# Contracting a bias matmul over 33 partitions instead of 128, in a fused cross-attention and expert kernel

## The reference, cut to what matters

```python
q = (layernorm(x) @ Wq + bq).reshape(1, B * N, H, hd)     # 1024 tokens, 16 heads of 32
kv = (cond @ Wkv + bkv).reshape(1, -1, 2, H, hd)          # 2048 context tokens
k, v = kv[:, :, 0], kv[:, :, 1]
q, k = _fq_sym(q * scale, axis=-1), _fq_sym(k, axis=-1)   # rounded to 255 levels
v = _fq_sym(v, axis=2)
attn = _fq_unsigned(softmax(q k^T))
x = x + (attn @ v) @ Wp + bp
x = x + sum over 8 experts of weight_e * ((silu(xn @ Wg_e) * (xn @ Wu_e)) @ Wd_e)
```

## Time and profile before

| | us |
|---|---|
| median of 3 runs | 724.55 |
| lowest and highest of the 3 | 721.7, 725.01 |
| the profiled execution, its own time | 725.01 |
| its span, first to last instruction | 723.2 |

### The profile page before, as it was taken

One profiled execution on the slowest core, in us unless ns is written; L12 is line 12 of the kernel. 1 busy time (PEld: TensorE's weight loads), 2 busy tenths in 40 slices (PEclk: granted clock), 3 DMA queues, 4 the chain that ended last, 5 costly groups with the idle time before them and its releaser, 6 DMA issues.

```text
span 723.2 us, 15795 instructions
## 1 busy us (share of the span) xinstructions
PE 618.9 (86%) x5307; PEld 328.3 (45%) x5307; DVE 567.9 (79%) x926; ACT 462.1 (64%) x559; POOL 402.8 (56%) x455
## 2 busy tenths in 40 slices
PE   6999999666867777777777688799999999999995
PEld 3444444233434333443434356455555555555543
DVE  4998888999999999999999998783646547465430
ACT  6344459789979989898989898343434334344321
POOL 5255458537587878787877874234334453344503
PEclk9999999999999999999999999899999999999998
DMA  7777857999989999999999999269697787967914
GB/s 254 198 148 176 182 135 145 182 190 194 173 165 198 184 198 193 188 192 189 189 189 185 200 176 170 88 213 212 162 253 161 225 221 176 242 157 225 145 27 58
DMA packets 318516, 129.42 MB, mean 179 GB/s; under 512 B 293508, under 2 KB 293508, under 8 KB 318472
## 3 DMA queue, kind: packets, MB, share of 16 engines
q1 hardware_dynamic: 311296, 112.64, 72.8%
q0 software_dynamic: 7168, 16.26, 11.0%
q10 hardware_dynamic: 8, 0.01, 0.0%
HBM read 44.33 MB, written 12.06 MB: 78 GB/s over the span
## 4 chain that ended last, share of the span: by engine, by line
PE 46%; issue 14%; DVE 11%; POOL 8%; DMA 7%; ACT 7%; SPq 5%; POOLq 1%; another core or an unknown queue 0%; ACTq 0%; DVEq 0%
PE psum L1668 43%; DMA work<-work 7%; ACT work L1065 4%; DVE spare L1400 3%; POOL work L672 3%; DVE spare L1391 2%; SPq L483 2%; SPq L481 2%; POOL exp_bias L678 1%; PE psum L1987 1%; SPq L450 1%; ACT work L967 1%; POOL work L657 1%; POOL bias_hl L636 1%; POOL out_dram L846 1%
## 5 line engine op out<-in xcount | busy, mean ns | idle before, releaser
L1065 ACT ACTIVATE work<-spare,exp_bias 128x2048 uint8<-128x2048 f32 (+1 forms) x127 | 253.2, 1995 | 29.3 <-POOL exp_bias L678 21.8
L1400 DVE TENSOR_SCALAR_CACHE_REDUCE spare<-psum,q_step_now 128x1024 f32<-128x1024 f32 x128 | 162.8, 1279 | 2.7 <-PE psum L1839 2.5
L672 POOL CAST work<-work 128x2048 int16<-128x2048 uint8 x70 | 132.3, 1890 | 39.2 <-DMA work<-work 35.4
L1391 DVE TENSOR_SCALAR_CACHE_REDUCE spare<-psum,q_step_now 128x2048 f32<-128x2048 f32 x64 | 150.6, 2353 | 0.1
L1839 PE MATMUL psum<-keys_region,work 128*128 128x512 f16 x256 | 73.1, 385 | 43.0 <-DVE spare L1400 27.1
L834 POOL DMA_INDIRECT work<-x_rows,slot_tok x32 | 49.8, 1558 | 88.5 <-DVE slot_w L1600 75.1
L1839 PE MATMUL psum<-keys_region,bias_hl 128*128 128x512 f16 x256 | 70.6, 381 | 28.4 <-DVE spare L1400 22.9
L846 POOL DMA_INDIRECT out_dram<-keys_region,slot_tok x32 | 51.7, 1615 | 74.8 <-ACT keys_region L1160 67.8
L1798 PEld LDWEIGHTS psum<-values_region,work 128*128 128x128 f16 x2016 | 65.0, 96 | 36.5 <-POOL work L672 21.6
L1668 PE MATMUL psum<-work,spare 128*128 128x480 f16 (+1 forms) x396 | 80.5, 364 | 0.0
L1798 PE MATMUL psum<-values_region,work 128*128 128x32 f16 x2016 | 70.0, 177 | 10.8 <-POOL work L672 7.0
(11 more groups left out here) (250 smaller groups left out, 1005.4 us busy)
## 6 DMA issues: line engine op xcount, KB each, us to landing
spare<-in_L_ffn_Wd_dram SPq DMA_DIRECT2D x8, 1024.0 KB, 15.5
spare<-in_L_ffn_Wg_dram SPq DMA_DIRECT2D x7, 1024.0 KB
spare<-in_L_ffn_Wu_dram SPq DMA_DIRECT2D x7, 1024.0 KB, 10.3
work<-in_ctx_dram SPq DMA_DIRECT2D x3, 1024.0 KB, 5.8
work<-work SPq DMA_TRANSPOSE x174, 3.7
token_region<-in_L_xattn_Wkv_dram SPq DMA_DIRECT2D x2, 1024.0 KB, 6.1
resid<-in_x_dram SPq DMA_DIRECT2D x2, 1024.0 KB, 8.9
out_dram<-work SPq DMA_DIRECT2D x8, 256.0 KB, 2.6
```

Source lines behind the costliest of these rows:

```text
L672: nc.gpsimd.tensor_copy(p_T_int[h % 4], pair_bytes[h % 4]).then_inc(unpacked, 1)
L1065: nc.scalar.activation(p_out, scores, ACT.Exp, bias=exp_bias[:, h % 4:h % 4 + 1], scale=-1.0, accum_out=p_sum[:, h:h + 1]).then_inc(exp_do ...
L1391: nc.vector.tensor_scalar(staged[h % 4], psum[:, at:at + 4, :].rearrange("p b k -> p (b k)"), q_step_now[:, h:h + 1], None, ALU.mult, ALU.min,
L1400: nc.vector.tensor_scalar(staged[h % 4][:, 1024 * c:1024 * c + 1024], psum[:, at:at + 2, :].rearrange("p b k -> p (b k)"), q_step_now[:, h ...
```

## The change

`add_bias` reads partitions 0 to 32 of both operands and leaves partitions 33 to 127 out. Nothing else is edited: the two operands are still cleared whole, `warm_up` still reads the whole of `bias_one`, and every semaphore stays where it was. The output still has 128 rows and 512 columns. What was added from the rows left out was zero times zero.

```diff
             def add_bias(out, n):
 
-                return nc.tensor.matmul(out, bias_one[:, :], bias_hl[:, n, :], start=False, stop=True)
+                return nc.tensor.matmul(out, bias_one[0:33, :], bias_hl[0:33, n, :], start=False, stop=True)
```

## The result

The changed kernel is slower: the ratio to the kernel before, over 8 runs of each, is 1.0063 with a 95% interval of 1.0035 to 1.0093. On the 725.08 us median of the kernel before that is 4.6 us, 2.5 to 6.7 by the interval. The medians themselves are 728.38 and 725.08 us, 3.3 us apart. The profiled execution took 731.33 us with a span of 729.6, which is the high end of its runs, as the profiled one of before was for the first three shown.

What follows compares the result with a forecast made beforehand. TensorE was taken to bound the front: 22 bias matmuls x 0.26 us, less 0.24 us of slack, gave 5.5 us, and 725.0 + 5.5 = 730.5 us. Its own range was 728.5 to 734; for 8 in 10, 722.5 to 735.

Steps and rivals of the forecast that it cites:

- What bounds the front: Before the attention, the chain of waits is nothing but TensorE, busy 80.70 of 80.70 us from 19.4 to 100.1.
- the route over query tile 5: End of the front: VectorE takes query tiles 4 and 5 at 117.37 us, with 0.07 us of slack after tile 5's bias.
- Streaming and load at no price: Bias matmuls: streaming stays at 0.216 us for 512 columns, and a shorter load, hidden already, gains nothing; 0 for streaming.
- The crossing: Way in and out of each 33-row matmul among 128-row ones: 0 to 0.52 us extra, 0.26 us taken.
- The sign that the prediction gave: In the front's chain, a bias matmul takes 0.22 + 0.26 us, its load no longer starting while the matmul before streams.
- The count: Biases ended by 117.30 us: 16 of keys, 6 of queries, 22 in all; 22 x 0.26 - 0.24 = 5.5 us.
- The sum: Whole kernel: the profiled 725.0 us plus 5.5 us of delay gives 730.5 us, 0.8% above the median of three runs.
- x: Extra time per narrow bias matmul for its two crossings, between 0 and 0.52 us, taken as 0.26 us.
- A: Rival at the bias matmuls: no price for the crossing, under some 0.03 us each, time 725.0 us; chance 0.38.
- B: Rival at the bias matmuls: two full restarts, 0.41 to 0.52 us each, time 733.8 to 736.2 us; chance 0.11.
- C: Rival in the front: chain leaves TensorE at the key tiles, 16 biases count, 3.9 us, time 728.9; chance 0.07.
- D: Rival in the experts: faster, a shift moves the 1.2 GHz stretches, up to 2.4 us back, 722.6 us; chance 0.05.

Runs made afterwards that it cites:

- one-column kernel: The 24 bias matmuls keep 128 rows but stream 1 column instead of 512, against the kernel before: ratio 1.0005, first scores 0.20 us sooner.
- doubled wide matmul: The wide bias matmul (128 rows) is issued twice in a row, against the kernel before: ratio 1.0067, first scores 4.76 us later.
- queries-only kernel: 33 rows for the 8 query biases, 128 for the 16 key biases, against the kernel before: ratio 1.0046, first scores 1.12 us later.

## Why the prediction was right, point by point

**What bounds the front.** Right in the direction that mattered: 22 matmuls of known cost, added, came through as 4.76 us. It was half of the truth. That the chain in the front is nothing but TensorE holds up to 92.29 us only; from there it ran over VectorE and ScalarE. The prediction found the route over query tile 5 by its 0.07 us of slack, and for work that is added this was enough. For work that is taken away it isn't: VectorE is idle for 80.70 - 73.33 = 7.4 us of the key stage, and the one-column kernel still brought the value maxima only 0.4 us forward. A busy share is no slack, since VectorE's operations wait for their tiles and for ScalarE.

**Streaming and load at no price.** A second narrow matmul costs 0.22 us in the chain, the same as a wide one, and the 33-row load takes 93 ns in place of 98. Both held.

**The crossing.** The forecast was 0.26 us for the two crossings of a bias matmul, between bounds of 0 and 0.52. It is 0.21, split nearly evenly, so the term was over-sized by a quarter. The prediction's middle was argued from one full restart of 0.20 us; what is there is two partial ones of 0.10 and 0.11, each less than the 0.163 us of overlap between records, which was the prediction's first step above nothing. That the middle of two bounds fell so near is luck: no row told 0.26 from any other value between them. The sign that the prediction gave held in the main, since each load starts 0.01 us ahead of its matmul and no longer 0.21; but to the letter the narrow load at 27.52 still starts while the record in front, which ends at 27.60, runs.

By the Trainium skill, page TensorEngine Tiling (Array Packing), Key Properties, a change of tiling mode drains TensorE. The same page of the Trainium skill, under When to Use Tiling, puts a contraction of up to 64 into row tiling. The traces agree with the place, since 64 rows pay and 65 do not, and with the rule that only the change counts, since a second narrow matmul pays nothing. They put the price at about 0.10 us each way, well under what two full restarts would give.

**The count.** 22 bias matmuls up to query tile 5. The third L1317 waits for exactly that one and starts 4.33 us later; 22 x 0.21 - 0.24 = 4.4. The 0.17 us that were allowed for the first 19 us are there too: from the second bias matmul to the third it is 8.84 us for 8.81, so 0.03 arrives and not 0.21. The first scores come 4.62 later, 0.3 of it on VectorE behind the third L1317. The doubled wide matmul confirms the 22 independently, within about one.

**The sum.** 5.5 us were forecast; 4.62 are measured at the first scores, 4.6 by the ratio of the runs and 3.3 by their medians. The size of x makes 22 x 0.05 = 1.1 us of the difference, and VectorE's 0.3 goes the other way. The 730.5 us were counted from the profiled run of 725.0. The median of 728.38 is 2.1 us below them, inside the range for 8 in 10 and just under the forecast's own 728.5 to 734. That this outcome was named over no price at all, by 0.39 to 0.38, was nearly a toss: the rows at hand couldn't decide it.

**The rivals.** A (no price) would be the case with 65 rows. B (two full restarts) is out by the 0.21. C (only keys) is out by the queries-only kernel, whose first scores come 1.12 us later. It had the route of the kernel before right, over ScalarE's rounding, but 0.07 us beside it lay a route with seven more bias matmuls, and the price lifts that one above it. D didn't happen, and no run showed anything near 0.5% of gain.

**What can't be settled here.** The profiled execution of the changed kernel is 1.7 us longer behind L1391 than that of the kernel before. Kernels that share this part lie up to 4.4 us apart there, in no order with their edits. The two at the ends are also those with the lowest and the highest mean granted clock of the whole execution: 0.977 in the changed kernel (601.8 us) and 0.993 with queries only (597.4 us); between them there is no order. So I put no part of it down to the change.

## What to carry to other kernels

A matmul with few rows of data between full ones should read zero rows along with them: up to 128 or to 65 rows cost nothing here, and reading 64, 33 or 1 row cost 0.21 us each time, as much as one more full matmul. If narrow matmuls are needed, put them next to one another, so that one pair of crossings serves several. And before taking work off an engine that is busy without a hole, ask what follows when it gets faster: here two routes were within 0.1 us of each other, adding cost in full and removing brought nothing. The chain of waits, read all the way through the stage, together with the slack of the route beside it, shows such a tie; the busy shares don't.

## What the runs showed of the hardware that was not expected

- The price of a narrow matmul is a step: none at 65 rows (0.22 us in the chain), all of it at 64, 33 and 1 (0.32 us, and 0.11 more in the product that follows).
- A crossing takes the head start from the next load (0.21 us before, 0.01 after) without waiting for the end of the last record, which is modelled: the load starts at 27.52, the record in front ends at 27.60.
- A [128 x 16] VectorE operation of 0.17 us was seen at 0.27 to 1.11 us in the same place of the program in other kernels; in four of them it ended within 0.03 us of the end of a POOL operation.
